# A decoder block on one core: the attention's output product from rounded parts of probabilities and rotated values, split on VectorE

## Chip, cores and metric

The kernel runs on one core of one Trainium2 chip. The metric is the device time of one execution in microseconds (us); the time of a version is the median of its runs.

## The reference, cut to what matters

Three blocks follow one another on x of 8 batches x 128 tokens x 512 features, each with a residual sum and a layer norm: a polynomial block with a gated product, a cross attention, and a last gated product. The change lies in the attention: 32 heads of width 128, keys and values from a context of 8 x 128 rows, and a mask that says which keys count.

```python
x = _rmsnorm(hidden_states, ln_weight)
h_q = (x @ w_q.T).reshape(b, lq, H, DH)
h_k = (key_value_states @ w_k.T).reshape(b, lk, H, DH)
h_v = (key_value_states @ w_v.T).reshape(b, lk, H, DH)
score = jnp.einsum('bqhd,bkhd->bhqk', h_q, h_k)
score = score + position_bias[None]
score = jnp.where(m, score, -jnp.inf)
score = jax.nn.softmax(score, axis=-1)
score = jnp.where(m, score, 0.0)
attn = jnp.einsum('bhqk,bkhd->bqhd', score, h_v).reshape(b, lq, H * DH)
out = attn @ w_out.T
return hidden_states + out
```

The mask of these inputs lets only keys count that lie among the last 32 of each batch. The kernel finds that out at run time and takes the branch `few`; all that is said here of the attention is of this branch.

## The kernel before, in words

The five engines run programs of their own, in order, and wait for one another through semaphores. The batch is worked in two halves of four batches (`HB`), so the attention runs over 2 x 32 = 64 head steps `n` (`HN`); a step treats one head for the four batches of a half.

All of a step's products are spread over a software pipeline. In iteration `n` of the attention loop TensorE does, in this order:

- `queries(n + 5)` (L600): the query weight times the keys, into `bank[0]`;
- `turn(n - 1)` (L658): transposes the probabilities of head n - 1 into `bank[3]`; waits for `prob_ok`, the end of `divide(n - 1)` on VectorE;
- `weigh(n - 2)` (L713): the output product of head n - 2, four products, one for each batch, with 32 rows of the array each, from `prob_t` and `u_sb` into `acc[0..3]`;
- `keys(n + 6)` (L581) into `bank[1]`, `values(n)` (L674) into `bank[3]`;
- `outer(n - 1)` (L691): values times output weight ("rotated values") into `bank[1]`; it waits until the keys have been copied out of this bank;
- where n % 4 is 2 or 3, half of `group_scores` (L613, L632), the scores of the next group of four heads, into `bank[2]`. With n % 4 equal to 2 the bias product (L613) comes first.

ScalarE copies the results out in the order `copy_queries(n + 5)` (L978), `copy_turned(n - 1)` (L986, to `prob_t`), `exponentials(n)` (L993), `copy_keys(n + 6)` (L971), `copy_values(n)` (L1000), `copy_outer(n - 1)` (L1007, to `u_sb`).

VectorE does in iteration `n`: `divide(n - 1)` (L1315 to L1321: row sums, their inverse, the scaling of the probabilities), `add_mask` (L1293, for n % 4 = 0 ahead of and behind the maximum, for n % 4 = 1 twice behind it), `find_max(n)` (L1299, L1301), and for the 24 iterations 4 to 27 `look_at` (L1307, L1309), a scan of the last block's weights. In iterations 33 and 34 it also adds the first half's result to the residual (L1157) and takes its statistics (L1164, L1167), in 25, 26, 62 and 63 there are transposes of features (on VectorE L1084 for the last two). Keys are made up to iteration 57, queries up to 58.

An iteration is told below from the start of its `turn` to the start of the next one's. Its kind is n % 4: kind 2 has the bias and eight scores' products behind `outer`, kind 3 the other half of the scores, kinds 0 and 1 have nothing there.

Outside the attention, the kernel already multiplies in a rounded format (`F32R`): ScalarE rounds an operand to it (`tile_hi`, L876), VectorE subtracts this from the whole (`tile_lo`, L1084, helper `low`), and TensorE adds two or three products of the parts (L461). The attention's products before the change take plain `F32` operands; each such product shows in the trace as two MATMUL instructions, a rounded one as one.

Of the kernel before, what the change touches and what calls it, by code (L numbers as in the profile page):

```python
# [29 lines left out]
P = 128  # L30
# [57 lines left out]
def decoder_kernel(nc, xT, ctxT, ctxF, x_tok, mask, consts, ad, a1, b1, ax, wqn, wvh, bx, bias, w3, out):  # L88
    with ExitStack() as ctx:
# [28 lines left out]
        ak, wo = two("ak", [P, 2 * C * P]), two("wo", [P, D])  # L118
        u_sb = two("u_sb", [P, D])

        tile_hi, tile_lo = two("tile_hi", [P, N], F32R), two("tile_lo", [P, N], F32R)

        gated = sb("gated", [P, N])
# [12 lines left out]
        prob = two("prob", [P, HB, P])  # L136
        prob_t = two("prob_t", [P, N])
        bias_sb = two("bias_sb", [P, GH * P])
# [51 lines left out]

        k_ok, t_ok, v_ok, u_ok = sem("k_ok"), sem("t_ok"), sem("v_ok"), sem("u_ok")
        added_ok, neg_max_ok, exp_ok = sem("added_ok"), sem("neg_max_ok"), sem("exp_ok")
        shifted_ok, sum_ok = sem("shifted_ok"), sem("sum_ok")
        inv_ok, prob_ok, turned_ok = sem("inv_ok"), sem("prob_ok"), sem("turned_ok")
        xn_ok = sem("xn_ok")
        mask_ok, key_scale_ok = sem("mask_ok"), sem("key_scale_ok")
# [259 lines left out]
        def _(pe):  # L456
# [112 lines left out]
            def attention(few):  # L569
                def keys(n):  # L570

                    half, par = n // HEADS, n % 2
                    pe.wait_ge(ak_dma[par], 16 * (n // 2 + 1))
                    if n == 0:
                        pe.wait_ge(hidden_ok, HALVES * F1)
                    else:
                        pe.wait_ge(k_ok, n)
                    if n > LEAD_K + 1:
                        pe.wait_ge(u_ok, n - LEAD_K - 1)
                    for c in range(C):  # L580
                        mm = pe.matmul(bank[1][:, 0:P] if few else bank[1][:], ak[par][:, (C + c) * P:(C + c + 1) * P],  # L581
                                       few_ctx[half][:, c * P:(c + 1) * P] if few else ctx_raw[half][:, c * N:(c + 1) * N],
                                       start=(c == 0), stop=(c == C - 1))
                    mm.then_inc(k_mm, 1)
# [98 lines left out]
                def outer(n):  # L683
# [8 lines left out]
                    else:  # L692
                        pe.wait_ge(turned_ok, n + 1)
                        for b in range(HB):
                            mm = pe.matmul(bank[1][:, b * P:(b + 1) * P], v_sb[par][:, b * P:(b + 1) * P],
                                           prob_t[par][:, b * P:(b + 1) * P], start=True, stop=True)
                    mm.then_inc(u_mm, 1)

                def weigh(n):
# [3 lines left out]
                    begins, ends = n % HEADS == 0, n % HEADS == HEADS - 1  # L703
                    pe.wait_ge(turned_ok, n + 1)
                    pe.wait_ge(u_ok, n + 1)
                    if not few:
                        pe.wait_ge(wo_dma[par], 16 * (n // 2 + 1))
                    for b in range(HB):
                        if begins:
                            pe.wait_ge(acc_read, (half + 1) * TT + b + 1)  # L710
                        if few:
                            rows = slice(b * FEW, (b + 1) * FEW)
                            mm = pe.matmul(acc[b][:], prob_t[par][rows, 0:P], u_sb[par][rows, :], start=begins, stop=ends,  # L713
                                           skip_group_check=True)
                        else:
                            mm = pe.matmul(acc[b][:], u_sb[par][:, b * P:(b + 1) * P], wo[par][:], start=begins, stop=ends,
                                           skip_group_check=True)
                        if ends and b < HB - 1:
                            mm.then_inc(acc_full, 1)
                    mm.then_inc(out_used, 1)  # L720
# [52 lines left out]

                pe.wait_ge(u_ok, HN)
                up(A30 % 2, 0, HALVES * F1)
# [70 lines left out]
        def _(act):  # L846
# [134 lines left out]
            def copy_turned(n):  # L981

                act.wait_ge(turned_mm, n + 1)
                if n >= 2:
                    act.wait_ge(out_used, n - 1)
                act.activation(prob_t[n % 2][:], bank[3][:], ACT.Copy).then_inc(turned_ok, 1)  # L986

# [14 lines left out]
            def copy_outer(n):  # L1002

                act.wait_ge(u_mm, n + 1)
                if n >= 2:
                    act.wait_ge(out_used, n - 1)
                act.activation(u_sb[n % 2][:], bank[1][:], ACT.Copy).then_inc(u_ok, 1)  # L1007

# [33 lines left out]
            split_b(T30, T30 % 2)  # L1042
            act.wait_ge(hidden_ok, s0 + 1)
            tile_from(T30, T30 % 2, hidden[T30 % 2])
            step3(1, 1, 0)
# [35 lines left out]
        def _(dve):  # L1081
# [214 lines left out]
            def find_max(n):  # L1296
# [5 lines left out]
                                  ALU.add).then_inc(shifted_ok, 1)  # L1302

            def look_at(k, par):

# [22 lines left out]
            for n in range(-LEAD_K, HN):  # L1328
                if n >= 1:
                    divide(n - 1)  # L1330
                if n >= 0:
# [5 lines left out]
                    if n % GH == 1:  # L1337
                        add_mask(n + 1)
                        add_mask(n + 2)
                if GH <= n < GH + SCANS:  # L1340
                    look_at(n - GH, n % 2)
# [3 lines left out]
                if n >= FEATURES_2:  # L1345
                    chunk(2, 2 * (n - FEATURES_2), bank[0])
                    chunk(2, 2 * (n - FEATURES_2) + 1, bank[0])
                if n == 1 - LEAD_K:
                    residual(1)
# [13 lines left out]

            divide(HN - 1)
            split_a(A30 + 1, (A30 + 1) % 2)
            product(A30, s0, T30, T30 % 2, True, 0)
# [131 lines left out]
```

## Time and profile before

| what | value |
|---|---|
| median of 3 runs | 802.4 us (802.1 to 803.47) |
| the profiled execution | 801.79 us |
| its span, first to last instruction | 799.7 us |
| TensorE busy | 758.4 us (95%) |
| VectorE busy | 484.9 us (61%) |
| ScalarE busy | 401.4 us (50%) |
| mean granted TensorE clock | 0.994 |
| first and last `turn` of the attention | at 253.0 and 657.3 us |

Busy time is the union of an engine's instructions. Matmuls are pipelined, and the end of each is modelled, so the starts of the following instructions say more of a product's cost than its own duration. In a timeline a row gives the start, the time covered, the engine, the line, the operation and, in brackets, how long the engine had stood idle before and what released it.

### The profile page before, as it was taken

What the parts mean: (1) busy time and instruction counts of PE and PEld (TensorE: products, weight loads), DVE (VectorE), ACT (ScalarE), POOL (GpSimd) and SP (SyncE); (2) the same over time, 40 slices, a digit from 0 to 9 for tenths busy, and PEclk for the clock granted to TensorE, in tenths of its full rate; (3) what the DMA queues carried; (4) which work ended last, traced back from release to release, by engine and by line L of the source; (5) the groups of instructions that cost most, each with busy time, mean ns of one, the idle gap of its engine ahead of it and who ended that gap; (6) DMA issues with size and microseconds to landing.
All of it is one profiled execution on the core that took longest, in us unless ns stands there. A gap on an engine that the chain in (4) does not pass through costs nothing.

```text
span 799.7 us, 12363 instructions
## 1 busy us (share of the span) xinstructions
PE 758.4 (95%) x4320; PEld 581.8 (73%) x4320; DVE 484.9 (61%) x821; ACT 401.4 (50%) x614; POOL 92.3 (12%) x86
## 2 busy tenths in 40 slices
PE   6999999999978999999999999999999879998994
PEld 5888888888867776777677767777777546886883
DVE  5654377533435668866785576554575647668656
ACT  5343233333335556655675566655665454464452
POOL 2010000270044000000000041000000000403503
PEclk9999999999999999999999999999999999999998
DMA  8462322432536778877885667666775332442641
GB/s 334 124 233 93 118 80 66 132 100 98 198 123 207 242 263 268 290 246 260 276 288 188 208 218 233 212 199 210 234 250 161 92 119 81 158 158 80 210 131 53
DMA packets 59751, 144.57 MB, mean 181 GB/s; under 512 B 6720, under 2 KB 6736, under 8 KB 59056
## 3 DMA queue, kind: packets, MB, share of 16 engines
q1 hardware_dynamic: 58112, 136.21, 52.3%
q0 software_dynamic: 1360, 7.23, 2.3%
q8 instruction: 35, 0.57, 0.3%
q10 hardware_dynamic: 224, 0.39, 0.2%
q14 instruction: 20, 0.16, 0.1%
HBM read 141.71 MB, written 2.10 MB: 180 GB/s over the span
## 4 chain that ended last, share of the span: by engine, by line
PE 82%; DVE 11%; issue 2%; ACT 2%; DMA 1%; POOL 1%; DVEq 0%; ACTq 0%; POOLq 0%
PE bank L461 25%; PE acc L461 16%; PE bank L632 7%; PE acc L713 7%; PE bank L581 6%; PE bank L691 6%; PE bank L674 5%; PE bank L600 5%; PE bank L613 4%; DVE score L1293 2%; DVE prob L1321 1%; DVE row_sum L1315 1%; DVE piece_top L1309 1%; DVE neg_max L1299 1%; PE bank L493 1%
## 5 line engine op out<-in xcount | busy, mean ns | idle before, releaser
L461 PE MATMUL bank<-feat_hi,a_hi 128*128 128x512 f32 x352 | 139.0, 395 | 10.2 <-DVE feat_lo L1084 7.4
L461 PE MATMUL bank<-feat_lo,a_hi 128*128 128x512 f32 x352 | 137.8, 392 | 0.0
L1084 DVE TENSOR_TENSOR a_lo<-a_raw,a_hi 128x1024 fp32r<-128x1024 f32 (+1 forms) x45 | 55.4, 1232 | 124.2 <-ACT a_hi L859 118.2
L978 ACT ACTIVATE t_ring<-bank 128x512 f32<-128x512 f32 x64 | 70.2, 1097 | 105.7 <-PE bank L600 105.7
L1315 DVE TENSOR_REDUCE row_sum<-prob 128x4 f32<-128x512 f32 x64 | 43.7, 683 | 90.4 <-ACT prob L993 90.0
L581 PEld LDWEIGHTS bank<-few_ctx,ak 128*128 128x128 f32 x512 | 62.8, 193 | 44.8 <-issue 42.5
L461 PE MATMUL acc<-b_hi,tile_hi 128*128 128x512 f32 x224 | 87.7, 392 | 3.6 <-issue 1.9
L461 PE MATMUL acc<-b_hi,tile_lo 128*128 128x512 f32 x224 | 87.2, 389 | 0.0
L461 PEld LDWEIGHTS bank<-feat_hi,a_hi 128*128 128x128 f32 x352 | 66.6, 189 | 27.4 <-issue 9.9
L632 PEld LDWEIGHTS bank<-t_ring,xn 128*128 128x128 f32 x512 | 62.7, 193 | 28.4 <-issue 28.4
L600 PEld LDWEIGHTS bank<-k_ring,wq 128*128 128x128 f32 x512 | 64.8, 192 | 18.5 <-issue 13.4
L581 PE MATMUL bank<-few_ctx,ak 128*128 128x128 f32 x512 | 74.4, 289 | 3.0 <-DMA ak<-ax 1.4
L461 PEld LDWEIGHTS bank<-feat_lo,a_hi 128*128 128x128 f32 x352 | 66.7, 189 | 13.5
L713 PE MATMUL acc<-u_sb,prob_t 32*128 32x512 f32 x512 | 73.0, 639 | 0.8 <-ACT u_sb L1007 0.8
L461 PE MATMUL bank<-feat_hi,a_lo 128*128 128x512 f32 x184 | 72.3, 393 | 0.0
L600 PE MATMUL bank<-k_ring,wq 128*128 128x128 f32 x512 | 68.5, 277 | 3.3 <-ACT k_ring L971 3.3
L1293 DVE TENSOR_TENSOR score<-bank,mask_add 128x512 f32<-128x512 f32 x64 | 42.5, 685 | 47.1 <-PE bank L632 47.1
L691 PE MATMUL bank<-wo,v_sb 128*128 128x512 f32 x128 | 69.5, 624 | 0.0
L674 PE MATMUL bank<-few_ctx,wv 128*128 128x128 f32 x512 | 68.1, 276 | 0.7 <-ACT prob_t L986 0.7
L876 ACT ACTIVATE tile_hi<-pair 128x512 fp32r<-128x512 f32 x54 | 34.0, 629 | 64.4 <-DVE pair L1111 37.2
L674 PEld LDWEIGHTS bank<-few_ctx,wv 128*128 128x128 f32 x512 | 62.3, 192 | 4.0 <-issue 4.0
L632 PE MATMUL bank<-t_ring,xn 128*128 128x128 f32 x512 | 62.6, 275 | 0.0
(108 smaller groups left out, 1106.4 us busy)
## 6 DMA issues: line engine op xcount, KB each, us to landing
ak<-ax SPq DMA_DIRECT2D x64, 512.0 KB, 3.9
wq<-wqn SPq DMA_DIRECT2D x64, 256.0 KB, 4.2
wv<-wvh SPq DMA_DIRECT2D x64, 256.0 KB, 3.4
wo<-bx SPq DMA_DIRECT2D x64, 256.0 KB, 4.0
a_raw<-w SPq DMA_DIRECT2D x22, 512.0 KB, 3.8
a_raw<-a SPq DMA_DIRECT2D x21, 512.0 KB, 4.1
b_raw<-b SPq DMA_DIRECT2D x34, 256.0 KB, 2.7
pair<-w SPq DMA_DIRECT2D x24, 352.0 KB, 4.5
```

The lines of the kernel that those rows point to most:

```text
L461: mm = pe.matmul(out_ap, w, x, start=start and k == 0, stop=stop and k == len(products) - 1, skip_group_check=True)
L581: mm = pe.matmul(bank[1][:, 0:P] if few else bank[1][:], ak[par][:, (C + c) * P:(C + c + 1) * P], few_ctx[half][:, c * P:(c + 1) * P] if f ...
L600: mm = pe.matmul(bank[0][:, c * P:(c + 1) * P], wq[par][:, c * P:(c + 1) * P], k_ring[:, n % RING, 0:P], start=True, stop=True)
L632: mm = pe.matmul(bank[2][:, b * P:(b + 1) * P], xn[half][:, c, b * SEQ:(b + 1) * SEQ], t_ring[g % 2][:, c, b, :, :].rearrange("p k h -> p ...
L674: mm = pe.matmul(bank[3][:, 0:P], wv[par][:, c * P:(c + 1) * P], few_ctx[half][:, c * P:(c + 1) * P], start=(c == 0), stop=(c == C - 1))
L691: mm = pe.matmul(bank[1][:], v_sb[par][:, 0:P], wo[par][:], start=True, stop=True)
L713: mm = pe.matmul(acc[b][:], prob_t[par][rows, 0:P], u_sb[par][rows, :], start=begins, stop=ends, skip_group_check=True)
L876: act.activation(tile_hi[par][:], src, ACT.Copy).then_inc(tile_hi_ok, 1)
L978: act.activation(t_ring[n // GH % 2][:].rearrange("p c b k h -> p (c b k h)")[:, n % GH:GH * N:GH], bank[0][:], ACT.Copy).then_inc(t_ok, 1)
L1084: return dve.tensor_tensor(out_ap, whole, high, ALU.subtract)
L1293: dve.tensor_tensor(score[n % GH][:], bank[2][:].rearrange("p (b k) -> p b k", b=HB), mask_add[j][:, half * HB:(half + 1) * HB, :], ALU.ad ...
L1315: dve.tensor_reduce(row_sum[:], prob[n % 2][:], AX_X, ALU.add).then_inc(sum_ok, 1)
```

## The change

The probabilities and the rotated values are each held as a rounded part and a rest. For the probabilities both parts are made by VectorE (`split_turned`), from `prob_t`, which is now single; for the rotated values ScalarE writes the rounded part (`copy_outer`, to `u_hi`) and VectorE the rest (`outer_rest`), straight from `bank[1]`. The product of each batch is then three products of parts (rounded x rounded, rounded x rest, rest x rounded), in rounded format, twelve instructions in place of eight. `u_hi` and `u_lo` are other names of `tile_hi` and `tile_lo`, so that ScalarE waits for the product before (`b_used`) ahead of the first two and for `out_used` behind the attention. The branch `few` = false, which does not run here, is changed too.

```diff
--- before.py
+++ after.py
@@ -116,9 +116,11 @@
         ctx_raw, few_ctx = two("ctx_raw", [P, C * N]), two("few_ctx", [P, C * P])
         xn = two("xn", [P, C, N])
         ak, wo = two("ak", [P, 2 * C * P]), two("wo", [P, D])
-        u_sb = two("u_sb", [P, D])
+        p_hi, p_lo = two("p_hi", [P, P], F32R), two("p_lo", [P, P], F32R)
 
         tile_hi, tile_lo = two("tile_hi", [P, N], F32R), two("tile_lo", [P, N], F32R)
+
+        u_hi, u_lo = tile_hi, tile_lo
 
         gated = sb("gated", [P, N])
         pair0, pair1 = sb("pair0", [P, 2 * N]), sb("pair1", [P, 2 * N])
@@ -134,7 +136,7 @@
         v_sb = two("v_sb", [P, N])
         score = [sb(f"score{i}", [P, HB, P]) for i in range(GH)]
         prob = two("prob", [P, HB, P])
-        prob_t = two("prob_t", [P, N])
+        prob_t = sb("prob_t", [P, N])
         bias_sb = two("bias_sb", [P, GH * P])
         mask_words = sb("mask_words", [P, BATCH, SEQ // 4], U32)
         mask_u8 = mask_words[:].bitcast(U8)
@@ -188,11 +190,11 @@
         silu_ok, hidden_ok = sem("silu_ok"), sem("hidden_ok")
         poly_ok, ratio_in, ratio_ok = sem("poly_ok"), sem("ratio_in"), sem("ratio_ok")
 
-        k_ok, t_ok, v_ok, u_ok = sem("k_ok"), sem("t_ok"), sem("v_ok"), sem("u_ok")
+        k_ok, t_ok, v_ok, u_hi_ok, u_lo_ok = sem("k_ok"), sem("t_ok"), sem("v_ok"), sem("u_hi_ok"), sem("u_lo_ok")
         added_ok, neg_max_ok, exp_ok = sem("added_ok"), sem("neg_max_ok"), sem("exp_ok")
         shifted_ok, sum_ok = sem("shifted_ok"), sem("sum_ok")
         inv_ok, prob_ok, turned_ok = sem("inv_ok"), sem("prob_ok"), sem("turned_ok")
-        xn_ok = sem("xn_ok")
+        p_hi_ok, p_lo_ok, xn_ok = sem("p_hi_ok"), sem("p_lo_ok"), sem("xn_ok")
         mask_ok, key_scale_ok = sem("mask_ok"), sem("key_scale_ok")
         few_dma, ctx_dma = sem("few_dma"), sem("ctx_dma")
         many_ok, keys_flag_ok = sem("many_ok"), sem("keys_flag_ok")
@@ -576,7 +578,7 @@
                     else:
                         pe.wait_ge(k_ok, n)
                     if n > LEAD_K + 1:
-                        pe.wait_ge(u_ok, n - LEAD_K - 1)
+                        pe.wait_ge(u_lo_ok, n - LEAD_K - 1)
                     for c in range(C):
                         mm = pe.matmul(bank[1][:, 0:P] if few else bank[1][:], ak[par][:, (C + c) * P:(C + c + 1) * P],
                                        few_ctx[half][:, c * P:(c + 1) * P] if few else ctx_raw[half][:, c * N:(c + 1) * N],
@@ -693,7 +695,7 @@
                         pe.wait_ge(turned_ok, n + 1)
                         for b in range(HB):
                             mm = pe.matmul(bank[1][:, b * P:(b + 1) * P], v_sb[par][:, b * P:(b + 1) * P],
-                                           prob_t[par][:, b * P:(b + 1) * P], start=True, stop=True)
+                                           prob_t[:, b * P:(b + 1) * P], start=True, stop=True)
                     mm.then_inc(u_mm, 1)
 
                 def weigh(n):
@@ -701,22 +703,25 @@
 
                     half, par = n // HEADS, n % 2
                     begins, ends = n % HEADS == 0, n % HEADS == HEADS - 1
-                    pe.wait_ge(turned_ok, n + 1)
-                    pe.wait_ge(u_ok, n + 1)
+                    pe.wait_ge(p_lo_ok, n + 1)
+                    pe.wait_ge(u_lo_ok, n + 1)
                     if not few:
                         pe.wait_ge(wo_dma[par], 16 * (n // 2 + 1))
-                    for b in range(HB):
-                        if begins:
-                            pe.wait_ge(acc_read, (half + 1) * TT + b + 1)
-                        if few:
+                    terms = [(p_hi, u_hi), (p_hi, u_lo), (p_lo, u_hi)] if few else [(u_hi, wo), (u_lo, wo)]
+                    for k, (left, right) in enumerate(terms):
+                        for b in range(HB):
+                            if begins and k == 0:
+                                pe.wait_ge(acc_read, (half + 1) * TT + b + 1)
                             rows = slice(b * FEW, (b + 1) * FEW)
-                            mm = pe.matmul(acc[b][:], prob_t[par][rows, 0:P], u_sb[par][rows, :], start=begins, stop=ends,
-                                           skip_group_check=True)
-                        else:
-                            mm = pe.matmul(acc[b][:], u_sb[par][:, b * P:(b + 1) * P], wo[par][:], start=begins, stop=ends,
-                                           skip_group_check=True)
-                        if ends and b < HB - 1:
-                            mm.then_inc(acc_full, 1)
+                            done = ends and k == len(terms) - 1
+                            if few:
+                                mm = pe.matmul(acc[b][:], left[par][rows, :], right[par][rows, :], start=begins and k == 0, stop=done,
+                                               skip_group_check=True)
+                            else:
+                                mm = pe.matmul(acc[b][:], left[par][:, b * P:(b + 1) * P].bitcast(F32), right[par][:],
+                                               start=begins and k == 0, stop=done, skip_group_check=True)
+                            if done and b < HB - 1:
+                                mm.then_inc(acc_full, 1)
                     mm.then_inc(out_used, 1)
 
                 def features(p, c, src, done):
@@ -771,7 +776,7 @@
                         head_scores(n + 1)
 
 
-                pe.wait_ge(u_ok, HN)
+                pe.wait_ge(u_lo_ok, HN)
                 up(A30 % 2, 0, HALVES * F1)
                 weigh(HN - 1)
 
@@ -981,9 +986,10 @@
             def copy_turned(n):
 
                 act.wait_ge(turned_mm, n + 1)
-                if n >= 2:
-                    act.wait_ge(out_used, n - 1)
-                act.activation(prob_t[n % 2][:], bank[3][:], ACT.Copy).then_inc(turned_ok, 1)
+                if n >= 1:
+                    act.wait_ge(p_lo_ok, n)
+                    act.wait_ge(u_mm, n)
+                act.activation(prob_t[:], bank[3][:], ACT.Copy).then_inc(turned_ok, 1)
 
             def exponentials(n):
 
@@ -1004,7 +1010,9 @@
                 act.wait_ge(u_mm, n + 1)
                 if n >= 2:
                     act.wait_ge(out_used, n - 1)
-                act.activation(u_sb[n % 2][:], bank[1][:], ACT.Copy).then_inc(u_ok, 1)
+                else:
+                    act.wait_ge(b_used, T30)
+                act.activation(u_hi[n % 2][:], bank[1][:], ACT.Copy).then_inc(u_hi_ok, 1)
 
             for n in range(-LEAD_K, HN):
                 if 0 <= n + LEAD_T < HN:
@@ -1041,6 +1049,7 @@
             split_a(A30 + 1, (A30 + 1) % 2)
             split_b(T30, T30 % 2)
             act.wait_ge(hidden_ok, s0 + 1)
+            act.wait_ge(out_used, HN)
             tile_from(T30, T30 % 2, hidden[T30 % 2])
             step3(1, 1, 0)
             step3(2, 2, 0)
@@ -1301,6 +1310,20 @@
                 dve.tensor_tensor(score[n % GH][:], score[n % GH][:], neg_max[:].unsqueeze(2).broadcast_to([P, HB, SEQ]),
                                   ALU.add).then_inc(shifted_ok, 1)
 
+            def split_turned(n):
+
+                dve.wait_ge(turned_ok, n + 1)
+                if n >= 2:
+                    dve.wait_ge(out_used, n - 1)
+                dve.tensor_copy(p_hi[n % 2][:], prob_t[:, 0:P]).then_inc(p_hi_ok, 1)
+                dve.wait_ge(p_hi_ok, n + 1)
+                low(p_lo[n % 2][:], prob_t[:, 0:P], p_hi[n % 2][:].bitcast(F32)).then_inc(p_lo_ok, 1)
+
+            def outer_rest(n):
+
+                dve.wait_ge(u_hi_ok, n + 1)
+                low(u_lo[n % 2][:], bank[1][:], u_hi[n % 2][:].bitcast(F32)).then_inc(u_lo_ok, 1)
+
             def look_at(k, par):
 
                 dve.wait_ge(piece_dma[par], k * 8 + (16 - 8 * par))
@@ -1337,6 +1360,8 @@
                     if n % GH == 1:
                         add_mask(n + 1)
                         add_mask(n + 2)
+                if n >= 1:
+                    split_turned(n - 1)
                 if GH <= n < GH + SCANS:
                     look_at(n - GH, n % 2)
                 if n == GH + SCANS:
@@ -1345,6 +1370,8 @@
                 if n >= FEATURES_2:
                     chunk(2, 2 * (n - FEATURES_2), bank[0])
                     chunk(2, 2 * (n - FEATURES_2) + 1, bank[0])
+                if n >= 1:
+                    outer_rest(n - 1)
                 if n == 1 - LEAD_K:
                     residual(1)
                 if n == 2 - LEAD_K:
@@ -1362,6 +1389,8 @@
                      f + (s0 + h * F3), last_block=True, f=f, split_next=split_next, after=after)
 
             divide(HN - 1)
+            split_turned(HN - 1)
+            outer_rest(HN - 1)
             split_a(A30 + 1, (A30 + 1) % 2)
             product(A30, s0, T30, T30 % 2, True, 0)
             split_b(T30, T30 % 2)
```

The helper that both new functions call is unchanged:

```python
def low(out_ap, whole, high):
    return dve.tensor_tensor(out_ap, whole, high, ALU.subtract)
```

## Rows read from the trace of the kernel before

**Rows 1.** The page's busy table and the granted clock in 40 slices.
```profile
PE 758.4 (95%) x4320; PEld 581.8 (73%) x4320; DVE 484.9 (61%) x821; ACT 401.4 (50%) x614; POOL 92.3 (12%) x86
PEclk9999999999999999999999999999999999999998
```

**Rows 2.** Two groups of four iterations, each cut at a `turn` of kind 3; columns first.
```profile
core 0: us, PE busy (x) PEld busy (x) DVE busy (x) ACT busy (x) POOL busy (x), PEclk, DMA share, GB/s
501.15:526.45 25.30, 25.30 (x176) 18.53 (x175) 14.61 (x28) 15.29 (x24) 0.00 (x0) 1.00 0.71 219
318.32:344.52 26.20, 25.84 (x176) 18.70 (x175) 19.61 (x36) 15.44 (x24) 0.00 (x0) 1.00 0.80 266
```

**Rows 3.** Timeline of the first of these groups: kind 0 and kind 1.
```profile
507.24 0.69 DVE L1293 TENSOR_TENSOR score<-bank,mask_add 128x512 f32<-128x512 f32 x1 [2.02 <-PE bank L632]
...
507.93 0.28 PE L658 MATMUL bank<-ident,prob 128*128 128x128 f32 x1
...
509.56 0.62 ACT L993 ACTIVATE prob<-score 128x512 f32<-128x512 f32 x1
...
512.93 0.28 PE L658 MATMUL bank<-ident,prob 128*128 128x128 f32 x1
...
513.14 1.14 PE L713 MATMUL acc<-u_sb,prob_t 32*128 32x512 f32 x8
...
514.21 1.16 PE L581 MATMUL bank<-few_ctx,ak 128*128 128x128 f32 x8
...
516.10 1.10 PE L691 MATMUL bank<-wo,v_sb 128*128 128x512 f32 x2
...
517.03 1.05 PE L600 MATMUL bank<-k_ring,wq 128*128 128x128 f32 x8
...
517.23 0.60 ACT L1007 ACTIVATE u_sb<-bank 128x512 f32<-128x512 f32 x1 [0.34 <-PE bank L691]
...
517.92 0.28 PE L658 MATMUL bank<-ident,prob 128*128 128x128 f32 x1
```

**Rows 4.** Timeline of iteration 62, with two products of features.
```profile
644.35 1.02 PE L691 MATMUL bank<-wo,v_sb 128*128 128x512 f32 x2
644.55 0.60 ACT L905 ACTIVATE feat_hi<-bank 128x512 fp32r<-128x512 f32 x1 [0.58 <-PE bank L493]
645.18 0.69 DVE L1084 TENSOR_TENSOR feat_lo<-bank,feat_hi 128x512 fp32r<-128x512 f32 x1 [1.38 <-ACT feat_hi L905]
...
647.66 0.39 PE L658 MATMUL bank<-ident,prob 128*128 128x128 f32 x1 [2.28 <-DVE prob L1321]
```

**Rows 5.** A stretch of 20 us in the polynomial block, rounded products only.
```profile
100.00:120.00 20.00, 20.00 (x90) 16.57 (x89) 15.84 (x25) 6.98 (x11) 0.00 (x0) 1.00 0.24 80
```

**Rows 6.** VectorE's shortest two-operand instruction, by line over the whole trace.
```profile
L1319 DVE TENSOR_TENSOR row_inv<-row_inv,row_valid 128x4 f32<-128x4 f32 x64 | 10.4, 162 | 2.2
```

**Rows 7.** Timeline of two iterations with a scan, kinds 0 and 1.
```profile
327.07 0.52 DVE L1307 TENSOR_SCALAR pair<-pair 128x704 int32<-128x704 int32 x1
...
328.42 0.68 DVE L1315 TENSOR_REDUCE row_sum<-prob 128x4 f32<-128x512 f32 x1
...
335.89 0.39 PE L658 MATMUL bank<-ident,prob 128*128 128x128 f32 x1 [0.33 <-DVE prob L1321]
```

**Rows 8.** VectorE's extra work in iterations 33 and 34, timeline.
```profile
462.97 2.47 DVE L1157 SCALAR_TENSOR_TENSOR resid<-resid,acc 128x512 f32<-128x512 f32 x4
...
468.40 2.46 DVE L1164 BATCH_NORM_STATS2 stats<-resid 128x6 f32<-128x512 f32 x4
```

**Rows 9.** Iterations 58 to 63 as one stretch, cut at `turn`.
```profile
619.12:657.34 38.22, 31.16 (x186) 18.66 (x185) 22.22 (x43) 18.66 (x30) 0.00 (x0) 1.00 0.37 115
```

**Rows 10.** Stretches of 3.4 us around the attention's two ends.
```profile
230.20:233.60 3.40, 1.77 (x13) 1.58 (x14) 0.00 (x0) 1.54 (x2) 2.87 (x6) 1.00 0.81 277
233.60:237.00 3.40, 3.03 (x13) 2.44 (x12) 0.00 (x0) 1.27 (x2) 3.29 (x3) 0.50 0.46 145
644.80:648.20 3.40, 1.12 (x7) 0.42 (x9) 2.91 (x6) 1.07 (x3) 0.00 (x0) 1.00 0.00 0
```

## The prediction, made before the changed kernel was run

> **What bounds the kernel now.** The page's table comes first: TensorE is busy 95% of the span, at full clock but for the last slice [rows 1]. Then the attention, in groups of four iterations cut at a `turn`: 25.30 us without the scan, with TensorE busy in all of them, 26.20 us with it, TensorE 25.84 and VectorE 19.61 [rows 2]. So TensorE sets the pace, and with the scan VectorE already holds it up now and then (0.33 us ahead of one `turn`) [rows 7]. The timeline gives one iteration of kind 1 [rows 3]: `turn` at 512.93, `weigh` 0.21 later, `keys` 1.07 after that, `outer` at 516.10, `queries` at 517.03, next `turn` at 517.92. The iteration takes 5.00 us (517.92 - 512.93), 3.17 of them from `turn` to `outer`. Kind 0 takes 5.00 too (512.93 - 507.93); of the 25.30 the other two take 15.3, which I split by the code into 8.53 for kind 2 (bias and scores) and 6.78 for kind 3.
>
> What the change touches is the way back from `outer(n - 1)` to TensorE. Today ScalarE copies it from 517.23 to 517.83 [rows 3], and only `weigh` needs it, an iteration's first 0.2 us further on. `divide`, which frees `turn`, does not depend on it.
>
> **Part 1, the product on TensorE.** Removed: eight instructions, 514.21 - 513.14 = 1.07 us [rows 3]. Added: twelve rounded ones in three sets of four, each set on its four row groups. In the polynomial block a rounded product of 512 columns comes every 20 / 90 = 0.22 us [rows 5]. A plain one takes two instructions, and `outer`, one such product, takes 517.03 - 516.10 = 0.93, so 0.43 to 0.47 for an instruction [rows 3]. Two sets at 0.43 leave 0.21 of the 1.07 for filling and emptying the row groups. Three rounded sets: 3 x 0.227 + 0.21 = 0.89, a saving of 0.18. Bounds: 0.70 (no set gap), 1.10 (each set pays its own 0.1 and more). No row shows rounded products in row groups; if they ran one after another the twelve would take 12 x 0.227 + 0.21 = 2.93 (rival D).
>
> **Part 2, VectorE's new work.** `split_turned`: two instructions of 128 columns. Bounds 0.16 each (four columns [rows 6]) and 0.69 (512 columns [rows 4]); in proportion to the columns 0.29, with gaps 0.6 for both. `outer_rest`: 0.69, as the same helper from a bank to `feat_lo` [rows 4]. Together 1.3 us per iteration. In a group VectorE would be busy 14.61 + 5.2 = 19.8 of at least 25.3, with scan 24.8 of 26.2 [rows 2]: by load alone it fits, barely.
>
> **Part 3, where that work stands in the queue.** This decides. `outer_rest(n - 1)` is the last thing of VectorE's iteration n, and it waits for ScalarE's copy of `outer(n - 1)`, the last product of TensorE's iteration n. Behind it on VectorE stands `divide(n)`, whose exponentials have long been done, and `turn(n)` on TensorE waits for `divide(n)`; behind `turn(n)` stand `weigh`, `keys`, `values` and `outer(n)`. That is a loop of one iteration: turn, outer, ScalarE's copy, rest, divide, turn. The trace has nearly its length in iteration 62: ScalarE's `feat_hi` at 644.55, `feat_lo` on VectorE at 645.18, divide, `turn` at 647.66, with TensorE idle for 2.28 us [rows 4]. From ScalarE's start to `turn` that is 3.11 us. From `outer` to ScalarE's start: 517.23 - 516.10 = 1.13 [rows 3]. Loop: 3.17 - 0.18 + 1.13 + 3.11 = 7.23, say 7.25 us. TensorE has only `queries` and the end of `outer` under those 4.24 us, 1.8 us; in each iteration of kinds 0 and 1 it then stands idle for 7.25 - 4.82 = 2.4 us.
>
> By kind: kind 1, 7.25. Kind 0, 7.25 + 0.2: its `add_mask` and maximum come ahead of the exponentials (507.24 to 509.56, 2.3 us [rows 3], against 1.4), ScalarE's copy of the keys stands behind these, and `outer` needs that copy. Kind 2: TensorE has 8.53 - 0.18 = 8.35 us of work, which covers the loop. Kind 3: 6.60 us of work, so the loop's 7.25. A group: 7.45 + 7.25 + 8.35 + 7.25 = 30.3 us.
>
> The rest of VectorE's work hides in front of `outer_rest`, which can't start before `turn` + 4.7. In kind 1 with a scan it is maximum 1.4, two `add_mask` 1.3, split 0.6, scan 328.42 - 327.07 = 1.35 [rows 7]: done at 4.6. If the split took 0.16 + 0.16 nothing changes; at 0.69 + 0.69 those iterations get 0.7 longer, +4 us in five or six of them.
>
> **Sum, clock aside.** Iterations 4 to 27, six groups with scan: 6 x (30.4 - 26.2) = +25.2 (kind 2 takes 0.1 more there). Iterations 28 to 55: 7 x (30.3 - 25.3) = +35.0. Iterations 56 and 57: +2.45 + 2.25 = +4.7. Iterations 1 to 3: +2.3 (the first has no `weigh`). Iteration 33 has the residual's 2.47 us and 34 the statistics' 2.5 and more on VectorE [rows 8]; both stand behind `outer_rest` and ahead of `divide`, so in the loop: +3.3 beyond what the groups hold. Iterations 58 to 63, 38.22 us [rows 9]: without `keys` the loop is 6.26, and I get 7.0 + 3 x 6.26 + 8.0 + 10.1 = 43.9, +5.7. Behind it `up` waits for `outer_rest(63)`, +0.7, less 0.2: +0.5. Total +76.7.
>
> **The clock.** Before the attention's steady part the granted clock fell to 0.50, 1.2 GHz, for 3.4 us, after a stretch of 3.4 us in which TensorE was busy 1.77. In iteration 62 it stayed at 2.4 GHz through a stretch with 1.12 busy and an idle time of 2.28 [rows 4, 10]. The new idle times of 2.4 us come twice per group, 28 times, and four of 3.3 us come in iterations 59 to 62. With one case of each outcome I take half of the 28. A fall of 3.4 us at half clock costs up to 1.7, some of it idle anyway: 1.5 each. 14 x 1.5 + 4 x 1.3 = +26. Bounds: none (0), all (28 x 1.7 + 7 = +55).
>
> The Trainium skill ("TensorE: Matmul & The Clock Gate", Part 1) has the lower clock come back after idleness; read strictly the gaps here, with matmuls close on both sides, would not do it, and the time would be that of rival B. This trace doesn't quite agree: its one fall followed a stretch that was half busy [rows 10].
>
> **Forecast.** 801.79 + 76.7 + 26 = 904.5 against the profiled execution, whose 801.79 is 0.6 under the median of 802.4: 905 us.
>
> **Rivals.**
> A, the forecast (0.60): loop closed, clock falls at some gaps, 890 to 945.
> B (0.20): loop closed, clock holds: 802.4 + 76.7 = 879, 865 to 890 with `weigh` at 0.70 (-12) or 1.10 (+10). For it: iteration 62. Against it: the fall at 233.6.
> C (0.09): every gap brings a fall, or `weigh` and the split come out at their upper bounds too: 802.4 + 76.7 + 55 = 934 and up, most of it over 945.
> D (0.05): rounded products don't overlap in their row groups. `weigh` 2.93 in place of 0.89, in the loop: 63 x 2.04 = +128, some 1007. Against it: the plain ones overlap, eight in 1.07.
> E (0.03), the other side: the loop stays open, because the way from `outer` to `turn` is covered. It would have to take under 1.8 us (the 0.93 of `outer` and the 0.89 of `queries`) where I count 4.24; then only Part 1 counts: 802.4 - 64 x 0.18 = 791. That would need `divide` to pass the waiting `outer_rest`, and in iteration 62 it did not pass `feat_lo`.
> The remaining 0.03 lies elsewhere, slower.
>
> Measurement can tell about 0.2% from no change. Faster 0.02, within 0.01 (E with `weigh` at 1.07), slower 0.97. The range of 8 in 10 takes A and B and leaves out C's upper part, D and E: 865 to 945.
>
> **What the profile after would show.** `turn` (L658) released by VectorE's `prob` in three of four iterations, with TensorE idle ahead of it some 2.4 us for kinds 0 and 1 and 0.6 for kind 3; groups of about 30.3 us, plus what the clock takes; TensorE's share down to some 85%; `weigh` at 0.9 us; the rest of the rotated values at 0.69 us directly ahead of `row_sum`; the clock row with slices below full speed in the attention and nowhere else; the polynomial block and the last block unchanged. Wrong would be: TensorE without gaps (E), `weigh` near 3 us (D), the clock at 1.00 throughout (B), or VectorE, and not its queue order, full: then its busy share in a group would be near 100%, where I expect two thirds to 80%.

## The result and the profile after

| | us |
|---|---|
| median after (6 runs, 908.7 to 922.78) | 911.96 |
| median before (6 runs, 800.25 to 803.47) | 802.25 |
| ratio, 95% interval | 1.1365, 1.1328 to 1.1403 |
| forecast | 905, range 865 to 945 |

The profiled execution is the longest of the six (922.78 us), 11 us over the median, with more time at the lower clock (mean 0.94, the others 0.951 to 0.959); below, lengths of single iterations are read where the clock stands at 1.00.

The page's busy table and clock row, against [rows 1]:

```profile
PE 799.7 (87%) x4576; PEld 630.4 (69%) x4576; DVE 553.5 (60%) x1013; ACT 409.3 (44%) x614; POOL 91.8 (10%) x86
...
PEclk9999999999997999889998889999988978999998
```

TensorE is now busy 87% of the span and no longer the one that sets the pace alone. VectorE has 69 us more to do (553.5 against 484.9), but its share of the longer span has not risen (60%). The granted clock has notches in the attention's slices. Two groups of four iterations, cut at a `turn` of kind 3, with scan and without, against [rows 2]:

```profile
335.23:365.76 30.53, 25.57 (x192) 19.50 (x191) 23.99 (x49) 15.85 (x24) 0.00 (x0) 1.00 0.71 228
635.62:666.15 30.53, 25.57 (x193) 19.50 (x191) 18.72 (x41) 15.83 (x24) 0.00 (x0) 1.00 0.59 182
```

Both take 30.53 us, although VectorE has 24.0 us to do in one and 18.7 in the other. A loaded engine would not make them equal; a loop does. One iteration of kind 1 in the timeline, against [rows 3]:

```profile
344.98 0.22 DVE L1318 CAST p_hi<-prob_t 128x128 fp32r<-128x128 f32 x1
...
345.23 0.29 DVE L1093 TENSOR_TENSOR p_lo<-prob_t,p_hi 128x128 fp32r<-128x128 f32 x1
...
346.85 0.60 ACT L1015 ACTIVATE tile_hi<-bank 128x512 fp32r<-128x512 f32 x1 [0.46 <-PE bank L693]
347.48 0.69 DVE L1093 TENSOR_TENSOR tile_lo<-bank,tile_hi 128x512 fp32r<-128x512 f32 x1 [0.59 <-ACT tile_hi L1015]
...
348.08 0.68 DVE L1338 TENSOR_REDUCE row_sum<-prob 128x4 f32<-128x512 f32 x1
...
349.95 0.39 PE L660 MATMUL bank<-ident,prob 128*128 128x128 f32 x1 [2.25 <-DVE prob L1344]
350.26 0.19 PEld L718 LDWEIGHTS acc<-tile_hi,p_hi 32*128 32x128 f32 x4
350.26 0.50 PE L718 MATMUL acc<-tile_hi,p_hi 32*128 32x512 f32 x4
...
351.17 1.16 PE L583 MATMUL bank<-few_ctx,ak 128*128 128x128 f32 x8
...
353.06 1.10 PE L693 MATMUL bank<-wo,v_sb 128*128 128x512 f32 x2
...
357.30 0.39 PE L660 MATMUL bank<-ident,prob 128*128 128x128 f32 x1 [2.25 <-DVE prob L1344]
```

ScalarE's copy starts at 346.85, VectorE's rest follows at 347.48, `divide` (L1338 and on) directly behind it at 348.08, and `turn` at 349.95 after 2.25 us in which TensorE stood idle. From ScalarE's start to `turn` it is 3.10 us. The product (L718) takes 351.17 - 350.26 = 0.91, from its start to that of `keys` (L583). The list of waits has this as TensorE's largest, us in total, times, longest:

```profile
PE bank L660 <- DVE prob L1344: 86.8, 49, 4.6
```

By kind, cut at each `turn`, kinds 2, 3, 0, 1:

```profile
596.62:605.08 8.46, 8.46 (x57) 6.12 (x58) 5.11 (x11) 3.02 (x5) 0.00 (x0) 1.00 0.42 132
605.08:612.32 7.24, 6.78 (x57) 5.58 (x55) 3.03 (x9) 4.23 (x7) 0.00 (x0) 1.00 0.56 181
612.32:619.80 7.48, 5.23 (x39) 3.91 (x39) 5.32 (x12) 4.49 (x7) 0.00 (x0) 1.00 0.69 232
619.80:627.16 7.36, 5.11 (x40) 3.91 (x40) 5.23 (x12) 4.10 (x6) 0.00 (x0) 1.00 0.66 187
```

Kinds 0 and 1, 5.00 us before, have lost nearly 2.5 each, kind 3 half a microsecond, and kind 2 is as good as before. The attention as a whole, first to last `turn`, and two stretches of 3.4 us of it:

```profile
250.68:775.32 524.64, 436.52 (x2915) 332.47 (x2916) 333.71 (x694) 247.62 (x376) 10.33 (x8) 0.91 0.54 173
```
```profile
513.50:516.90 3.40, 1.15 (x13) 0.79 (x16) 3.07 (x7) 1.55 (x3) 0.00 (x0) 1.00 0.65 224
516.90:520.30 3.40, 3.40 (x24) 2.75 (x17) 2.16 (x5) 1.34 (x3) 0.00 (x0) 0.50 0.56 152
```

In the first TensorE was busy 1.15 us, the rest of it in front of the `turn` at 516.17; in the next the clock is at 0.50, 1.2 GHz. The mean over the attention is 0.91 in this execution, the longest of the six.

### The profile page after: what moved, and what is told of

Read it like the earlier page. It is cut to its first block, busy times and chain, and to the rows that moved or that the text cites. A ratio compares the mean times of both kernels' runs of the same rounds, so it can differ in the third digit from the quotient of the medians.

```text
span 920.0 us, 13132 instructions
## 1 busy us (share of the span) xinstructions
PE 799.7 (87%) x4576; PEld 630.4 (69%) x4576; DVE 553.5 (60%) x1013; ACT 409.3 (44%) x614; POOL 91.8 (10%) x86
## 4 chain that ended last, share of the span: by engine, by line
PE 77%; DVE 14%; ACT 4%; issue 2%; DMA 1%; POOL 1%; ACTq 0%; DVEq 0%; POOLq 0%
PE bank L463 22%; PE acc L463 14%; PE bank L583 9%; PE bank L676 8%; PE acc L718 7%; PE bank L693 7%; DVE tile_lo L1093 4%; DVE prob L1344 4%; DVE row_sum L1338 3%; ACT tile_hi L1015 3%; PE bank L634 3%; PE bank L615 3%; PE bank L660 2%; PE bank L602 2%; PE bank L495 1%
## 5 line engine op out<-in xcount | busy, mean ns | idle before, releaser
L1093 DVE TENSOR_TENSOR tile_lo<-bank,tile_hi 128x512 fp32r<-128x512 f32 x66 | 45.6, 692 | 149.4 <-ACT tile_hi L1015 147.9
L660 PE MATMUL bank<-ident,prob 128*128 128x128 f32 x64 | 24.2, 379 | 86.8 <-DVE prob L1344 86.8
L583 PEld LDWEIGHTS bank<-few_ctx,ak 128*128 128x128 f32 x512 | 75.0, 225 | 25.8 <-issue 24.3
L583 PE MATMUL bank<-few_ctx,ak 128*128 128x128 f32 x512 | 88.0, 325 | 2.1 <-DMA ak<-ax 1.1
L676 PE MATMUL bank<-few_ctx,wv 128*128 128x128 f32 x512 | 82.2, 314 | 0.0
L660 PEld LDWEIGHTS bank<-ident,prob 128*128 128x128 f32 x64 | 12.6, 196 | 98.2 <-DVE prob L1344 98.1
L676 PEld LDWEIGHTS bank<-few_ctx,wv 128*128 128x128 f32 x512 | 77.0, 230 | 1.8 <-issue 1.8
L463 PEld LDWEIGHTS bank<-feat_lo,a_hi 128*128 128x128 f32 x352 | 67.1, 191 | 13.7
L693 PE MATMUL bank<-wo,v_sb 128*128 128x512 f32 x128 | 73.3, 657 | 0.0
L992 ACT ACTIVATE prob_t<-bank 128x512 f32<-128x512 f32 x64 | 39.3, 614 | 64.1 <-PE bank L660 64.1
```

The costliest lines, as they stand in the source:

```text
L463: mm = pe.matmul(out_ap, w, x, start=start and k == 0, stop=stop and k == len(products) - 1, skip_group_check=True)
L660: mm = pe.transpose(bank[3][:, 0:P], prob[n % 2][:].rearrange("p b k -> p (b k)")[:, j:N:GH], ident[:])
L676: mm = pe.matmul(bank[3][:, 0:P], wv[par][:, c * P:(c + 1) * P], few_ctx[half][:, c * P:(c + 1) * P], start=(c == 0), stop=(c == C - 1))
L693: mm = pe.matmul(bank[1][:], v_sb[par][:, 0:P], wo[par][:], start=True, stop=True)
L992: act.activation(prob_t[:], bank[3][:], ACT.Copy).then_inc(turned_ok, 1)
L1093: return dve.tensor_tensor(out_ap, whole, high, ALU.subtract)
```

## Experiments

Nine kernels were run. Those named "changed" start from the kernel after the change.

### The rest behind divide, and not ahead of it

```diff
                 if n >= 1:
                     divide(n - 1)
+                if n >= 2:
+                    outer_rest(n - 2)
...
-                if n >= 1:
-                    outer_rest(n - 1)
...
             divide(HN - 1)
+            outer_rest(HN - 2)
             split_turned(HN - 1)
```

> The same instructions as in the changed kernel; on VectorE the rest of the rotated values of head n - 1 stands behind divide(n) and not ahead of it, so the loop turn, outer, copy, rest, divide is open. If the order in VectorE's queue makes the loss, groups without scan fall from 30.5 to 25.6 us (a few tenths of waiting ahead of weigh), groups with scan, where VectorE then has 24.7 us of work and stalls between, to about 27.5, and the kernel to 818 us (810 to 828). If VectorE is simply overloaded by 1.3 us per iteration (rival), the order changes little: over 880. If the rounded product is the cause (rival): 912, no change.

Measured: 828.71 us, ratio 1.0340 (1.0314 to 1.0365). 83 of the 110 us are gone with not one instruction less. The groups with and without scan:

```profile
320.01:347.75 27.74, 25.30 (x192) 19.54 (x191) 23.64 (x48) 15.79 (x24) 0.00 (x0) 1.00 0.75 252
567.24:592.99 25.75, 24.86 (x192) 19.46 (x191) 18.93 (x40) 15.50 (x24) 0.00 (x0) 1.00 0.68 215
```

They are 27.74 and 25.75 against 27.5 and 25.6 expected. Now the two differ: the load on VectorE does count, once the loop is open. The timeline of kinds 0 and 1 with scan shows what is left:

```profile
387.64 0.68 DVE L1093 TENSOR_TENSOR tile_lo<-bank,tile_hi 128x512 fp32r<-128x512 f32 x1
...
387.77 0.39 PE L660 MATMUL bank<-ident,prob 128*128 128x128 f32 x1 [0.65 <-DVE prob L1344]
...
388.47 0.50 PE L718 MATMUL acc<-tile_hi,p_hi 32*128 32x512 f32 x4 [0.31 <-DVE tile_lo L1093]
```

`turn` still waits 0.65 us for a full VectorE, and the product, which comes right behind, 0.31 us for the rest. In kinds 1 and 2 the product so starts 0.7 to 0.8 us behind `turn` and not 0.2, in the groups without scan as well; that is why those take 25.75 us and not the 24.62 of the kernel without the rest, which comes next. The total is 11 us over the expectation and just outside its range. Most of it lies outside the groups: iterations 33 and 34 took 19.4 us against 14.4 before (6.8 us of them at half clock), and the last six 45.8 us against 38.2 before [rows 9], with 13.7 us at half clock. Of these, iteration 63 took 15.1 against 9.7: the rest of head 62, behind `divide(63)`, reached the product 2.5 us late, and the clock fell around it.

### No rest at all

```diff
-                    pe.wait_ge(u_lo_ok, n + 1)
+                    pe.wait_ge(u_hi_ok, n + 1)
...
-                if n >= 1:
-                    outer_rest(n - 1)
```

(the same exchange of semaphores for `keys` and `up`; `outer_rest` of the last head is left out too)

> The rest of the rotated values is not computed: the product reads what was left in u_lo. All else as in the changed kernel, the split of the probabilities and twelve rounded instructions included. If the loop through outer_rest makes the loss, nothing is left of it: the product's saving of 0.16 to 0.18 us in 64 iterations, -11, and +3 for the split where the scan fills VectorE: 794 us (788 to 800), groups without scan 24.6 us. If the rounded product or the split of the probabilities costs (rival): 830 or more. The clock stays at 1.00 in the attention.

Measured: 802.94 us, ratio 1.0012 (0.9998 to 1.0026). So `outer_rest` and its wait carry the whole loss, but the expected gain is not there either:

```profile
317.82:344.62 26.80, 25.17 (x193) 19.43 (x191) 21.32 (x44) 15.80 (x24) 0.00 (x0) 1.00 0.78 260
550.65:575.27 24.62, 24.62 (x192) 19.26 (x191) 16.22 (x36) 15.26 (x24) 0.00 (x0) 1.00 0.69 226
```

Without scan a group is 24.62, 0.68 less than [rows 2], just the product's 0.17 per iteration. With scan it is 26.80, 0.60 more: kinds 0 and 1 were already held by VectorE (5.19 and 5.60 us before, against 5.00 without scan), and the two instructions of `split_turned` (0.22 and 0.29 us) go almost whole into them. By `turn`s, iterations 27 to 57 gained 4.3 us; the gain is missing only in the group of iteration 33, which took 0.8 longer. Iterations 3 to 26 lost 3.0, the first two 0.6, with a fall of the clock, and the last six 2.0, with two. The rounded product and the split of the probabilities together were thus worth nothing measurable here.

### The gaps filled

```diff
                         queries(n + LEAD_T)
+                    if few and 2 <= n < HN and (j in (1, 2) or n > HN - LEAD_T - 1):
+                        pe.wait_ge(v_ok, n)
+                        for _ in range(7):
+                            pe.matmul(bank[3][:, 2 * P:3 * P], ident[:], ident[:], start=True, stop=True)
```

> The changed kernel with seven plain products of the identity with itself (128 columns, two instructions each, some 1.6 us) in the idle time ahead of turn in iterations whose n % 4 is 1 or 2, and in the last five; their result is never used. They lie in a gap of 2.4 us, so no wait gets shorter. If some 30 us of the loss are the lower clock, the clock stays at 1.00, each group takes 30.5 us and the kernel 881 us (876 to 888). If the lower clock costs nothing, or the gaps are not what brings it (rival): 905 to 920.

Measured: 887.03 us, ratio 1.1064 (1.1038 to 1.1091), mean clock 0.986 to 0.992. More work, 25 us less. The idle product with itself (L748, fourteen instructions) stands where nothing stood, and `turn` waits for the same `divide`:

```profile
347.13 1.73 PE L748 MATMUL bank<-ident 128*128 128x128 f32 x14
...
349.54 0.39 PE L660 MATMUL bank<-ident,prob 128*128 128x128 f32 x1 [0.68 <-DVE prob L1348]
```
```profile
327.48:358.00 30.52, 28.69 (x221) 22.63 (x219) 23.98 (x49) 15.91 (x24) 0.00 (x0) 1.00 0.69 229
610.98:641.52 30.54, 28.71 (x221) 22.66 (x219) 18.70 (x41) 15.91 (x24) 0.00 (x0) 1.00 0.58 182
```

Groups of 30.52 and 30.54 as in the changed kernel where its clock stood: the filling moves no wait. So the lower clock costs 911.96 - 887.03 = 25 us at least. The 6 us over the expectation are a fall that the filling did not prevent, in iterations 33 and 34 (6.8 us at 0.50, at a gap of which 3.07 us were left), one more in iteration 63 (3.4 us), and 1.6 us of filling that TensorE had no gap for in iteration 58.

### The product in the plain format again

```diff
-                    terms = [(p_hi, u_hi), (p_hi, u_lo), (p_lo, u_hi)] if few else [(u_hi, wo), (u_lo, wo)]
+                    terms = [(p_hi, u_hi)] if few else [(u_hi, wo), (u_lo, wo)]
...
-                                mm = pe.matmul(acc[b][:], left[par][rows, :], right[par][rows, :], ...
+                                mm = pe.matmul(acc[b][:], left[par][rows, :].bitcast(F32), right[par][rows, :].bitcast(F32), ...
```

> The changed kernel with the output product in the plain format again: rounded probabilities times rounded rotated values only, as F32 operands, eight instructions as before the change (the terms with the two rests are left out of the sum); both splits and all waits stay. The product then takes 1.07 us in place of 0.91 inside the loop: +0.16 in 62 iterations, 922 us (914 to 930), groups 31.1 without clock falls. If the rounded format itself is what slows the kernel (rival): clearly under 900.

Measured: 926.62 us, ratio 1.1551 (1.1520 to 1.1582), 15 us over the changed kernel. The rounded format is a gain inside the loop too. Kinds 2, 3, 0, 1:

```profile
601.43:610.06 8.63, 8.63 (x53) 5.94 (x54) 5.11 (x11) 3.02 (x5) 0.00 (x0) 1.00 0.45 133
610.06:617.47 7.41, 6.95 (x54) 5.40 (x52) 3.04 (x9) 4.24 (x7) 0.00 (x0) 1.00 0.55 177
617.47:624.99 7.52, 5.27 (x36) 3.72 (x36) 5.33 (x12) 4.53 (x7) 0.00 (x0) 1.00 0.65 220
624.99:632.50 7.51, 5.26 (x36) 3.71 (x36) 5.22 (x12) 4.10 (x6) 0.00 (x0) 1.00 0.61 190
```

Kinds 2, 3 and 1 are 0.17, 0.17 and 0.15 longer than after the change, kind 0 only 0.04: there `outer` waits for ScalarE's copy of the keys, and the product is off the path, as the prediction's 0.2 us for kind 0 says. The sum of these is 8 us; the other 7 I put down to the clock, without a run that shows it.

### The rest twice

```diff
+                low(spare[:], bank[1][:], u_hi[n % 2][:].bitcast(F32))
                 low(u_lo[n % 2][:], bank[1][:], u_hi[n % 2][:].bitcast(F32)).then_inc(u_lo_ok, 1)
```

> The changed kernel with the subtraction of outer_rest done twice on VectorE, the first time into a buffer that nobody reads: 0.61 us more in the loop, and nothing else. If the loop through VectorE sets the pace, kinds 0, 1 and 3 get 0.61 longer each (7.48 to 8.09, 7.34 to 7.95, 7.24 to 7.85) and kind 2 (8.47, TensorE's work, 1.1 us over the loop) does not change: some 47 x 0.61 = +29, and more or longer falls of the clock, +5 to +15: 945 to 955 us. If VectorE's load over the whole group set the pace (rival), kind 2 would get longer too, or in the groups without scan nothing would.

Measured: 952.72 us, ratio 1.1859 (1.1839 to 1.1879). Kinds 2, 3, 0, 1:

```profile
333.72:342.18 8.46, 8.46 (x58) 6.13 (x58) 6.46 (x13) 3.03 (x5) 0.00 (x0) 1.00 0.45 154
342.18:350.02 7.84, 6.78 (x58) 5.58 (x56) 5.54 (x13) 4.84 (x7) 0.00 (x0) 1.00 0.61 214
350.02:358.10 8.08, 5.23 (x40) 3.91 (x40) 7.25 (x15) 4.05 (x7) 0.00 (x0) 1.00 0.82 257
358.10:366.04 7.94, 5.09 (x39) 3.89 (x40) 7.14 (x15) 4.11 (x6) 0.00 (x0) 1.00 0.71 216
```

Three kinds are 0.58 to 0.60 longer, kind 2 not at all. That is the loop's signature: 0.6 us more on VectorE costs 0.6 us of time, except where TensorE's own work is longer than the loop. In some 47 iterations these are 28 of the 41 us; the other 13 I put down to the clock, without a run that shows it.

### What a better version would need

Four kernels look for one. The first is the changed kernel with the rest behind `divide`, the scans of kinds 0 and 1 moved to kinds 2 and 3, and the last iteration mended; the second moves the scans in the kernel before:

```diff
-                if GH <= n + 1 < GH + SCANS:
-                    load_piece(n + 1 - GH, (n + 1) % 2)
...
+                if n == GH - 1 or (GH <= n < GH + SCANS - 1 and n % GH >= 2):
+                    k = 0 if n < GH else n - GH if n % GH == 2 else n - GH + 1
+                    load_piece(k, 0)
+                    load_piece(k + 1, 1)
...
-                    look_at(n - GH, n % 2)
+                    k = n - GH
+                    if k % GH >= 2:
+                        first = k - 2 if k % GH == 2 else k - 1
+                        look_at(first, 0)
+                        look_at(first + 1, 1)
```

> The version with the rest behind divide, and two more moves: the scans of kinds 0 and 1, where VectorE sets the pace, done in kinds 2 and 3 (two each), and in the last iteration the rest of head 62 ahead of divide(63) again. If the remaining loss against the kernel before is VectorE's load in kinds 0 and 1, the six groups with scan fall from 27.75 to 25.8 us (-12) and iteration 63 from 15.1 to some 11 (-4): 812 us (807 to 817). If it is the clock or the tail alone (rival): 822 or more.

> The kernel before, with the scans of kinds 0 and 1 moved to kinds 2 and 3 and their loads with them. VectorE held kinds 0 and 1 at 5.19 and 5.60 us in the six groups with scan; TensorE's own work there is 5.00. Expected 6 x 0.9 = 5.4 less: 797 us (795 to 799). If two loads of a scan together hold up the weights' loads (rival): 801 or more.

Measured: 815.18 us, ratio 1.0159 (1.0141 to 1.0176), for the first; 796.98 us, ratio 0.9937 (0.9923 to 0.9951), for the second. Their groups with scan:

```profile
317.98:344.75 26.77, 25.36 (x193) 19.61 (x191) 23.79 (x48) 15.43 (x24) 0.00 (x0) 1.00 0.81 261
```
```profile
319.52:344.82 25.30, 25.30 (x176) 18.53 (x175) 19.92 (x37) 15.32 (x24) 0.00 (x0) 1.00 0.83 275
```

In the kernel before, the move brings the groups with scan to the 25.30 of the others, 5 us in all, and this is the one version here that computes the whole sum and beats both kernels. With the splits and the rest the groups don't come down to 25.8 (26.77): two scans and a split no longer fit into kind 3, and kind 0 takes 5.66 us, where it takes 4.83 without a scan. Iteration 63 came down from 15.1 to 11.4 us, as expected.

The other two give up the terms with the rests, so that no new work falls on VectorE:

```diff
-        u_sb = two("u_sb", [P, D])
+        u_sb = two("u_sb", [P, D], F32R)
...
-        prob_t = two("prob_t", [P, N])
+        prob_t = two("prob_t", [P, N], F32R)
```

> The kernel before with prob_t and u_sb in the rounded format, written so by ScalarE: one rounded product of four instructions in place of eight plain ones; the two terms with the rests are left out of the sum. No new work on VectorE, no new wait. If a set of four rounded instructions in row groups takes 0.23 and filling 0.21 us, weigh falls from 1.07 to 0.45; groups without scan from 25.3 to 22.9 (VectorE begins to hold kinds 0 and 1 at 4.4 to 4.6), groups with scan from 26.2 to 25.0: 776 us (770 to 784). If TensorE's work on the product is not what sets the pace (rival): 795 or more.

> Both of the last two: one rounded product (the terms with the rests left out) and the scans in kinds 2 and 3. Groups with scan should fall to those without, some 23 us, so -11 against the version with one rounded product: 765 us (758 to 773).

Measured: 784.03 us, ratio 0.9789 (0.9764 to 0.9815), and with the scans moved 775.98, ratio 0.9689 (0.9667 to 0.9711). Both gain, both less than expected. The product came out right, 502.16 - 501.72 = 0.44 us, 0.63 less than the plain one; the iterations did not. One of kind 1:

```profile
501.72 0.50 PE L713 MATMUL acc<-u_sb,prob_t 32*128 32x512 f32 x4
...
502.16 1.16 PE L581 MATMUL bank<-few_ctx,ak 128*128 128x128 f32 x8
...
503.64 0.60 ACT L971 ACTIVATE k_ring<-bank 128x512 f32<-128x512 f32 x1
...
504.35 1.08 PE L691 MATMUL bank<-wo,v_sb 128*128 128x512 f32 x2
```

Kinds 0 and 1 take 4.65 us, 0.35 less than before, and kinds 2 and 3 gain hardly more (0.36), so a group without scan takes 23.9 us and not 22.9. ScalarE's copy of the keys ends at 504.24, and `outer`, which needs that bank, starts 0.11 later. The keys' product ends at 503.32, but the copy starts only at 503.64, directly behind ScalarE's exponentials (in the kernel before, ScalarE had waited 0.23 us for that product). The next engine's queue has become the bound. That last step is read from the timeline and was not tried.

## Why the prediction was right

**The loop.** `outer_rest` ahead of `divide` in VectorE's queue closes a loop of one iteration. Undoing the order alone gives back 83 of 110 us, leaving the rest out gives back all, doing it twice costs 0.6 us in each kind that the loop rules. The equal groups with and without scan, and kind 2 unmoved by the second rest, refute an overloaded VectorE. The predicted 3.11 us from ScalarE's start to `turn`, taken from the features' products [rows 4], measured 3.10.

**The lengths.** 7.45, 7.25, 8.35 and 7.25 were forecast for kinds 0 to 3, 7.48, 7.36, 8.46 and 7.24 measured. Kinds 1 and 2 are 0.1 too short in the forecast: after standing idle TensorE starts the product 0.31 us behind `turn` (350.26 - 349.95) and not 0.21. TensorE idles 2.25 us where 2.4 was forecast, and 0.46 where 0.6 was. Of the four gaps of 3.3 us forecast for the end of the attention, the trace has three, of 3.14, and one of 1.35.

**The terms of TensorE.** `weigh` was put at 0.89 and took 0.91; rounded products do overlap in their row groups, rival D is out. (The 0.227 us for an instruction stands in no row: [rows 5] give 20 / 90 = 0.222, which makes 0.88.) The bounds of the split (0.16 to 0.69) held, the values by proportion (0.29) were 0.22 and 0.29. As forecast, the residual and the statistics in iterations 33 and 34 lie in the loop, between the rest and `divide`:

```profile
523.14 2.47 DVE L1166 SCALAR_TENSOR_TENSOR resid<-resid,acc 128x512 f32<-128x512 f32 x4
525.53 0.68 DVE L1338 TENSOR_REDUCE row_sum<-prob 128x4 f32<-128x512 f32 x1
...
535.75 2.46 DVE L1173 BATCH_NORM_STATS2 stats<-resid 128x6 f32<-128x512 f32 x4
```

**The sum.** Clock aside +76.7 was forecast. The filled version is 84.8 over the kernel before. Less its 1.6 of needless filling, and less some 4 (an estimate) for 10.3 us at half clock, it is 79. It is close to rival B, the loop with the clock held, made by hand: 887 measured, 879 forecast for B.

**The clock.** +26 was forecast, from "half of the gaps" at 1.5 us each; the filled version shows 25 at least, and with its own 4 us and 1.6 some 30. In the profiled execution, the granted clock fell at 14 of the 27 gaps of 2.25 us (and for 3.4 us in the last block, where none was forecast). Two iterations of kind 1, one with each length of fall:

```profile
317.90:326.76 8.86, 6.61 (x39) 5.26 (x39) 6.55 (x14) 4.10 (x6) 0.00 (x0) 0.81 0.62 196
380.48:390.77 10.29, 8.04 (x39) 6.12 (x39) 6.55 (x14) 4.10 (x6) 0.00 (x0) 0.67 0.57 193
```

Against 7.35 at full clock, a fall of 3.4 us costs the 1.5 that was forecast. But six of the 14 lasted 6.8 us and cost 2.9, which the forecast didn't have. So the direction and the price of a short fall came from the trace before; that one half, taken from one case of either outcome, came out so nearly was luck. The strict reading of the Trainium skill ("TensorE: Matmul & The Clock Gate", Part 1) that was set beside it, that the clock holds (rival B), does not agree with this case: the clock fell again and again at gaps of 2.25 us with products close on both sides, and filling the gaps kept it up.

**Where the forecast's parts failed** was in the experiments' expectations. Without the rest and with one rounded term, a gain of TensorE was counted in full where VectorE (groups with scan) or ScalarE (one rounded term) was nearly the bound already. With the rest behind `divide`, what was missed lay mostly in the iterations outside the groups, with their falls of the clock. The prediction's Part 1 is a saving of 0.18 per iteration, which alone would be 11 us; the kernel without the rest stood level with the one before. So rival E's price of 791 was too low as well: the kernel without the rest has less work than rival E's, and took 803.

## What to carry to other kernels

An instruction that waits for a late input holds up all that stands behind it in an in-order queue, so its price can be far above its own time: ask which of its inputs comes last, which instruction behind it was ready earlier, and who waits for that one. Here 0.69 us per iteration, 44 us of VectorE's time in all, cost 110 us in the wrong place, and a move behind its neighbour gave back 83. And when a kernel begins to wait in short gaps on TensorE, add the lower clock to the bill: it was a quarter of this loss.

## What the runs showed of the hardware

- Short gaps can lower TensorE's clock. With 2.25 us idle ahead of `turn` twice in 30.5 us the granted clock was 0.91 on average over the attention of the profiled execution, and it fell at 14 of 27 such gaps, for 3.4 or 6.8 us. With fourteen idle instructions in each of these gaps (0.68 left) it was 0.99 on average over the attention, with falls only in iterations 33 and 34, at a gap of 3.07, and in iteration 63, at one of 1.58.
- The six runs of the changed kernel took 908.7 to 922.8 us, with mean clocks of 0.959 to 0.940 in the same order; before the change it was 800.3 to 803.5. Gaps don't always bring such scatter: with the rest twice and gaps of 2.85 us, four runs took 951.6 to 953.3.
- Four rounded products of 512 columns on four row groups take 0.44 us with entry and exit, twelve 0.91, so 0.23 to 0.24 for each further set of four; eight plain instructions take 1.07.
- The output product starts 0.31 us behind its `turn` when TensorE had stood idle ahead of that `turn` (0.46 to 2.25 us after the change), 0.21 when it had not.
